# A 12-stage decoder kernel: the side steps of its first cross attention spread over more slots, and semaphores cleared by ranges

## What is computed

```python
q = (x @ Wq + bq).reshape(1, B * N, H, hd)            # B*N = 2048 queries
kv = (cond @ Wkv + bkv).reshape(1, -1, 2, H, hd)      # 512 keys
q, k, v = fq_sym(q * scale), fq_sym(k), fq_sym(v, over the keys)    # 8 bit, kept as floats
attn = softmax(q @ k.T)
attn = clip(round(attn / s), 0, 255) * s               # s = max(attn) / 255, by row
return (attn @ v) @ Wp + bp
```

## Time and profile before

| | us |
|---|---|
| median of 3 runs | 3998.09 (3995.31 to 3998.46) |
| the profiled execution | 3996.9 |
| its span, first to last instruction | 3995.1 |
| of it L0X, from the barrier before it to the one behind it | 277.2 to 664.0 |
| of that the loop, from its first maxima to its last | 307.2 to 643.6 |

### The profile page before, as it was taken

The page is one execution under the profiler, slowest core; times in us unless marked ns, Lnnn a source line. Parts: engine busy times, 40 slices in busy tenths (PEclk is TensorE's granted clock), DMA queues, the critical chain, the costliest instruction groups (busy, mean ns, idle before and its releaser), DMA issues. The chain is left out here.

```text
span 3995.1 us, 56226 instructions
## 1 busy us (share of the span) xinstructions
PE 3152.4 (79%) x17265; PEld 2306.4 (58%) x17296; DVE 2698.2 (68%) x8364; ACT 1820.2 (46%) x5598; POOL 467.9 (12%) x585
## 2 busy tenths in 40 slices
PE   7975554979999997764589974569999999999465
PEld 5653333747777775542267762237777777777344
DVE  4667875368878885668844457856666676666597
ACT  4546664135555552224411122346666666666243
POOL 0011110011111110111111110011111111111100
PEclk9995555989999998776689986679999999999588
DMA  1004555000000001000000012000000000000000
GB/s 57 1 23 88 96 94 143 1 14 1 1 1 1 1 1 40 0 4 26 1 16 1 1 44 103 1 11 1 1 1 1 1 1 1 1 1 1 33 1 22
DMA packets 141736, 83.72 MB, mean 21 GB/s; under 512 B 135424, under 2 KB 139648, under 8 KB 139776
## 3 DMA queue, kind: packets, MB, share of 16 engines
q1 hardware_dynamic: 141440, 80.14, 7.5%
HBM read 44.47 MB, written 2.10 MB: 12 GB/s over the span
## 5 line engine op out<-in xcount | busy, mean ns | idle before, releaser
L2213 DVE CUSTOM_DVE_ANT_0 L3A_masked<-ps,L3A_hidden,L3A_negrstd 128x128 f32<-128x128 f32 (+1 forms) x512 | 193.4, 415 | 322.7 <-PE ps L2104 233.4
L2162 ACT ACTIVATE L3A_probs<-L3A_masked,L3A_negmax 128x128 f32<-128x128 f32 (+1 forms) x512 | 228.8, 449 | 237.3 <-DVE L3A_negmax L2213 237.2
L332 PE MATMUL ps<-s_weights_b,s_XT 128*128 128x512 f32 (+1 forms) x640 | 301.1, 603 | 36.7 <-ACT s_XT L753 12.8
L2132 PE MATMUL ps<-s_weights_b,L3A_OT 128*128 128x256 f32 x1024 | 264.1, 381 | 14.5 <-DVE s_R L2242 14.5
L332 PE MATMUL ps<-s_weights_b,s_Xc 128*128 128x512 f32 x512 | 243.7, 598 | 7.4 <-DVE L3A_rot L2077 3.3
L879 ACT ACTIVATE L0X_pf<-ps,L0X_bias,L0X_qscale 128x512 int16<-128x512 f32 x256 | 197.1, 776 | 114.9 <-DVE L0X_bias L912 113.8
L2085 POOL TENSOR_TENSOR L3A_rstd<-L3A_ve,s_mhalf 128x4 f32<-128x4 f32 x144 | 145.0, 1007 | 852.5 <-DVE L3A_ve L2045 852.5
L332 PEld LDWEIGHTS ps<-s_weights_b,s_XT 128*128 128x128 f32 x640 | 124.0, 211 | 127.4 <-issue 69.3
L909 DVE TENSOR_REDUCE L0X_negmax<-ps 128x2 f32<-128x1024 f32 x128 | 156.1, 1219 | 60.7 <-PE ps L820 59.0
L2132 PEld LDWEIGHTS ps<-s_weights_b,L3A_OT 128*128 128x128 f32 x1024 | 175.1, 191 | 28.9 <-issue 15.7
L2162 ACT ACTIVATE L1A_probs<-L1A_masked,L1A_negmax 128x128 f32<-128x128 f32 (+1 forms) x256 | 114.3, 447 | 119.7 <-DVE L1A_negmax L2213 117.1
(11 more groups left out here) (512 smaller groups left out, 8635.4 us busy)
## 6 DMA issues: line engine op xcount, KB each, us to landing
s_weights_b<-w_L3A SPq DMA_DIRECT2D x1, 9984.0 KB, 26.7
s_weights_b<-w_L1A SPq DMA_DIRECT2D x1, 7936.0 KB, 21.5
s_weights_a<-w_L2F SPq DMA_DIRECT2D x1, 4224.0 KB, 12.9
s_weights_b<-w_L1F SPq DMA_DIRECT2D x1, 3840.0 KB, 11.9
s_weights_b<-w_L3F SPq DMA_DIRECT2D x1, 3136.0 KB, 10.9
s_weights_a<-w_L2A SPq DMA_DIRECT2D x1, 2898.0 KB, 9.6
s_weights_a<-w_L0F SPq DMA_DIRECT2D x1, 2176.0 KB, 8.8
s_X<-x SPq DMA_DIRECT2D x1, 2048.0 KB, 8.3
```

What stands on the lines that cost most here:

```text
L332: last = pe.matmul(out, lhs(k), rhs(k), start=(k == 0), stop=(k == n - 1))
L2132: last = pe.matmul(c.bank(3)[:, j * DM:(j + 1) * DM], OT[:, u % 4, j * P:(j + 1) * P], w["wo"][:, h, :], start=(h == 0 and j == 0), stop=( ...
L2162: last = a.activation(pr[:, u % 4, cols], ms[:, u % 2, cols], ACT.Exp, bias=nmx[:, h, j:j + 1], scale=-1.0, accum_out=sm[:, h, j:j + 1])
L2213: last = eng.tensor_tensor_reduce(out=ms[:, u % 2, cols], in0=s[:, cols], in1=hidden[:, P - j * P:2 * P], scale=-1.0 if gated else nrs[:, ...
```

## The change

Two things. First, `clear` gives GpSimd one instruction for each run of consecutive semaphore numbers, where it had one for each semaphore. Second, in L0X the steps Q and Y are cut in two, by tile of tokens: the first half (Q, Y) tells nobody, the second (Q+, Y+) stands in the next slot and tells VectorE, which does its part for both. All steps get other slots; T1 of a sequence moves into slot 0 of that sequence itself, and its scores wait for T0 only, and for T1 from their second tile on. `outputs` moves from slot 5 to 6, the scaling of the normalised rows from 13 to 15, and GpSimd's parts move accordingly.

```diff
             def _(pool):
-                for s in self.sems:
-                    pool.sem_clear(s)
+                numbers = sorted(s.num for s in self.sems)
+                first = numbers[0]
+                for n, after in zip(numbers, numbers[1:] + [None]):
+                    if after != n + 1:
+                        pool.sem_clear(range(first, n + 1))
+                        first = after
...
-    STEP_AT = {0: ("X", 1), 2: ("Q", 1), 6: ("oT", -1), 8: ("Y", -1), 10: ("T0", 1), 11: ("T1", 1)}
+    STEP_AT = {0: ("T1", 0), 2: ("X", 1), 4: ("Q", 1), 5: ("Q+", 1), 8: ("oT", -1), 10: ("Y", -1), 11: ("Y+", -1), 14: ("T0", 1)}
+    STARTS = ("Q", "Y")
...
-            elif what == "Q":
-                for j in range(TT):
-                    last = project(pe, halves[:, j, :], lambda k: c.XT[:, k, j * P:(j + 1) * P], lambda k: w["wq"][:, k, :])
+            elif what in ("Q", "Q+"):
+                j = len(what) - 1
+                last = project(pe, halves[:, j, :], lambda k: c.XT[:, k, j * P:(j + 1) * P], lambda k: w["wq"][:, k, :])
...
-            last.then_inc(side_made, 1)
+            if what not in STARTS:
+                last.then_inc(side_made, 1)
...
-                    if p % PAIRS == 0:
-                        pe.wait_ge(side_act, act_through(("T1", b)))
+                    if m == 0:
+                        pe.wait_ge(side_act, act_through((("T0", "T1")[j], b)))
...
-                    if i >= 0 and s % PAIRS == VALUE_LAG - 1:
+                    if i >= 0 and s % PAIRS == VALUE_LAG:
                         outputs(i)
-                    if i >= 0 and s % PAIRS == 13:
+                    if i >= 0 and s % PAIRS == 15:
                         S.vec_norm_scale(v, i + 1, i)
```

More of the change, by code:

```diff
@@ L641, in sublayer_l0_cross @@
     VALUE_LAG = 6
-    STEP_AT = {0: ("X", 1), 2: ("Q", 1), 6: ("oT", -1), 8: ("Y", -1), 10: ("T0", 1), 11: ("T1", 1)}
-    VEC_LATER = 1
-    steps = [("X", 0), ("Q", 0), ("T0", 0), ("T1", 0)]
+    STEP_AT = {0: ("T1", 0), 2: ("X", 1), 4: ("Q", 1), 5: ("Q+", 1), 8: ("oT", -1), 10: ("Y", -1), 11: ("Y+", -1), 14: ("T0", 1)}
+    STARTS = ("Q", "Y")
+    steps = [("X", 0), ("Q+", 0), ("T0", 0), ("T1", 0)]
     step_at = {}
@@ L649, in sublayer_l0_cross @@
             i = s // PAIRS + ahead
-            if 0 <= i < SEQS:
+            if 0 <= i < SEQS and (what, i) not in steps:
                 step_at[s] = (what, i)
-                steps.append((what, i))
+                if what not in STARTS:
+                    steps.append((what, i))
     number = {x: m for m, x in enumerate(steps)}
-    BY_ACT, BY_VEC = ("X", "T0", "T1", "oT"), ("Q", "Y")
+    BY_ACT, BY_VEC = ("X", "T0", "T1", "oT"), ("Q+", "Y+")
     def act_through(x):
@@ L721, in pe_side @@
             what, i = x
-            m = number[x]
+            m = number[(what + "+", i) if what in STARTS else x]
             if m:
@@ L742, in pe_side @@
             else:
-                for j in range(TT):
-                    last = project(pe, halves[:, j, :], lambda k: c.oT[:, k, j * P:(j + 1) * P], lambda k: w["wp"][:, k, :])
-            last.then_inc(side_made, 1)
+                j = len(what) - 1
+                last = project(pe, halves[:, j, :], lambda k: c.oT[:, k, j * P:(j + 1) * P], lambda k: w["wp"][:, k, :])
+            if what not in STARTS:
+                last.then_inc(side_made, 1)
         def act_side(a, x):
@@ L766, in vec_side @@
             e.wait_ge(side_made, number[x] + 1)
-            if what == "Q":
+            if what == "Q+":
                 if i:
@@ L841, in _ @@
                             lambda k: ctxT[:, k, :]).then_inc(v_made, 1)
-                for x in steps[:2]:
+                for x in (steps[0], ("Q", 0), steps[1]):
                     pe_side(pe, x)
@@ L956, in _ @@
                         steps_of(s - 2)
-                    if s - VEC_LATER in step_at:
-                        vec_side(v, step_at[s - VEC_LATER])
+                    if s - 1 in step_at:
+                        vec_side(v, step_at[s - 1])
                     i = s // PAIRS - 1
-                    if i >= 0 and s % PAIRS == VALUE_LAG - 1:
+                    if i >= 0 and s % PAIRS == VALUE_LAG:
                         outputs(i)
-                    if i >= 0 and s % PAIRS == 13:
+                    if i >= 0 and s % PAIRS == 15:
                         S.vec_norm_scale(v, i + 1, i)
@@ L991, in _ @@
                     i = s // PAIRS
-                    if s % PAIRS == 4 and i + 1 < SEQS:
+                    if s % PAIRS == 7 and i + 1 < SEQS:
                         pool_q(p, i + 1)
@@ L995, in _ @@
                         if i > 1:
-                            g.wait_ge(side_vec, vec_through(("Y", i - 2)))
+                            g.wait_ge(side_vec, vec_through(("Y+", i - 2)))
                         g.tensor_tensor(Xb[:], c.X[:, i * TT:(i + 1) * TT, :], over(w["bp"], TT), ALU.add).then_inc(xb_ready, 1)
-                    if i and s % PAIRS == 10:
+                    if i and s % PAIRS == 13:
                         S.pool_rstd(g, i - 1)
```

## The result

Medians in us, the two kernels side by side on one chip:

| | before | after |
| --- | --- | --- |
| median of 4 runs (lowest to highest) | 3996.83 (3995.31 to 3998.46) | 3928.7 (3925.62 to 3928.93) |
| span of the profiled execution | 3995.1 | 3923.8 |
| L0X, barrier to barrier | 386.4 | 360.7 |
| its loop, first maxima to last | 336.4 | 312.4 |
| the 23 gaps between sublayers, together | 67.8 | 23.7 |

A forecast was written before the change was run, and what follows sets the result against it. Bounds: in L0X, VectorE's work and its waits for scores; between sublayers, single clears with all other engines waiting. 46.6 (clears) + 19.5 (loop) = 66.1 us off the 3998.1 median gives 3932, within 3924 to 3942 (0.66).

The forecast's parts named there:

- The clears, 46.6 us: Semaphore clears between sublayers: 684 instructions become 46, so 638 go at 0.073 us each, gaining 46.6 us.
- a clear of many numbers takes what a clear of one does: Clears between sublayers: a clear of a range takes 44 ns however wide, so the full 46.6 us are gained.
- Rival 1: Clears cost by width: 27 ns per number gives 3949 us (chance 0.12); the full 0.073 us gives 3978 (0.04).
- The 73 ns for each clear: Blocks of clears: 24 more clears cost VectorE 1.75 us more idle time, 0.073 us each, all on the path.
- rival 2: At the clears: code fetched under them is now waited for, at most 28 us back, 3946 to 3960 (chance 0.05).
- The loop, 19.5 us: L0X: period from 44.2 to about 41.7 us, 18.5 over the loop; with start and rounding, 19.5 in all.
- the seven waits: L0X period: seven small VectorE waits, 0.3 to 1.2 us each, sum 5.6, in place of three of 2 to 3.
- I took 1.2 GHz for all halves: L0X, halves of Q and Y: TensorE's clock rises only at the end of Q+, so a half takes 1.8 us.
- granted clock still near 0.58: Sign for the profile after: the granted clock in the L0X loop stays near 0.58.
- Rival 4: L0X: TensorE runs the halves at 2.4 GHz, 0.95 us each; period 38.4, total 3908 us (chance 0.04).
- Other stages unchanged: Stages other than L0X: unchanged but for the barriers; the prediction calls itself wrong if another stage moves.
- VectorE's three waits for scores: L0X period before: VectorE waits 2.75 us behind Q, 2.62 behind Y, 2.08 behind T1, together 7.45.

## Where the prediction was right and where not

- **The clears, 46.6 us.** Measured 44.2 in the gaps, 45 by the kernel that has them alone. The term that was wrong is "a clear of many numbers takes what a clear of one does": it takes 129 ns at 17 and 259 at 41, and over the 46 clears that is 3.3 us more than 44 ns each. Rival 1 had the direction, but 27 ns for each number; the rows say about 5. From the other side came 0.8 us, since the time from the last clear to the next work got shorter at some places. The 73 ns for each clear held, but not as read: one clear follows the next after 71 ns, and in five of the 23 blocks one step takes 360 to 363 ns, which makes the mean 73. The two blocks of the earlier trace rows have no such step. What these pauses are no run shows; with ranges they are gone. At 17 numbers VectorE's idle time was to be 2.00 - 16 x 0.071 = 0.86 with a free width; the 0.09 of the wide clear make it 0.95, as measured. At 41 it is 3.75 less the 2.88 us of the single clears and plus the 0.38 of the three that replace them, 1.25, and 1.26 was measured.
- **Fetches.** The part around the clears stayed what it was in most places: 0.46 us from the last work to the first clear and 0.34 from the last clear to the next work, in the median of the 23 places, before and after. At three places the second part fell (0.68, 0.78 and 0.63 us before, 0.32 to 0.34 after). At two it grew: from 0.32 to 0.41 in this profile alone, and from 0.32 to 0.54 at the first of the two blocks of 17 clears, those of L3X, in all runs with this `clear`. There the last of the engines to reach the block's end is TensorE (instructions of L177 at this place, before and after):

```profile
L177 PEldq DRAIN  x1: 135/135/135, 3706.2 to 3706.2; - x1
```

```profile
L177 PEldq DRAIN  x1: 135/135/135, 3640.7 to 3640.7; - x1
```

In both it ends 0.42 us behind the start of the first clear. The 17 clears took 1.18 us and covered it; the one clear of 0.13 us does not. So something did come to light, as rival 2 said, but it is 0.22 us at one place and no fetch. What the Trainium skill's section on instruction fetch mechanics ("Runtime: NRT & Kernel Launch") speaks of is not seen at these places: had the 17 clears of the earlier trace rows covered a fetch, VectorE's idle time there would be longer than the 0.95 of the point above, and it is 0.95.
- **The loop, 19.5 us.** Measured 25.7 in the first profile and 22.3 in the second. All of the seven waits are where they were said to be: 0.40, 0.51, 0.72, 1.09 and 1.05 for 0.36, 0.44, 1.14, 0.91 and 1.11 (the third, behind Q, is the worst), and slots 6 and 12 with 0.82 each where the clock is as assumed. Then the period is 42.0 us for 41.7 forecast. The step that failed is "I took 1.2 GHz for all halves": in most periods the clock rises inside Q+ and Y+, which take 1.4 to 1.8 us for 2.07, and those two waits are 0.2 to 0.3. That makes the period 40.95, 0.75 less than forecast, and over the six whole periods 5.1 us, most of the 6.2 that the forecast had too little. The sign "granted clock still near 0.58" failed with it: it is 0.63. The rows had shown a rise behind 4.7 us of busy TensorE, and the step took that one place for the rule. Rival 4 named the mechanism, with too large a size: it had the first half fast as well.
- **`outputs`.** Named as a new cost of 0.91 us a period; it is 1.09, and taking it away gave some 11 us in all, 6 to 9 of them in L0X.
- **Other stages unchanged.** True in the sum (3533.0 to 3531.6), not stage by stage: L1A is 1.2 us shorter and L2X 1.1. By the prediction's own words ("I am wrong if another stage moves") that is a miss. It had no term for TensorE's clock in stages that the change doesn't touch, and these shifts come with it. That they nearly cancel in this kernel is luck; with the loop alone they are 6.6 us.
- **The total.** The forecast of 3932 is 3 us from the 3928.7 measured. The clears had 2.4 us too much and the loop 6.2 too little, so part of this closeness is luck.
- **What bounds the loop.** That VectorE's three waits for scores are what can be gained was the premise. The kernel without them is 55 us shorter in L0X than before and runs at VectorE's pace.

What the prediction didn't ask is whether halves or slots bring the gain. It listed the slots' savings (T1) and costs (`outputs`, X, slot 0) side by side, and by its own numbers they nearly cancel; the kernel with the new slots alone shows it. That the halves in the old slots take most of T1's wait away as well, so that the move of T1 is not needed for it, it did not see.

## What to carry to other kernels

A serial block between stages is worth counting: one instruction for each semaphore, 71 ns apart with four engines standing, was 1.2% of this kernel, and a clear by range costs 44 to 259 ns for any width seen here. In a loop that one engine paces, write down when each side step's input is ready and how long the step blocks the engine that feeds the pacing one. In this loop a step was free when it stood three slots behind the copy it needs and was short enough for TensorE's lead; a whole projection still cost up to 1.0 us there, and cut in two it cost nothing. And look at what a moved consumer now holds up: here one slot later for `outputs` gave back some 11 us.

## What was not expected of the hardware

- A semaphore clear by range costs 44 ns for 1 number, 47 to 53 for four, 64 for five and then about 5.4 ns for each more, up to 259 at 41. Single clears follow each other after 71 ns, but in five of the 23 blocks one step took 0.36 us.
- The clock was not to be foretold from TensorE's own rows here. In the changed kernel it rose inside the second half of a projection (0.50, then 0.77); in another execution of the very same kernel it stayed at 0.50 there for two periods; with the halves in the old slots, TensorE as busy, it stayed at 0.50 as well. In the kernel with whole steps in the best slots TensorE was busy nearly throughout from 373.84 us on, with one stop of 0.37 us, and was still at the lower level 7.9 us later (window of that stretch):

```profile
373.84:381.70 7.86, 7.49 (x52) 5.05 (x52) 7.37 (x17) 7.41 (x18) 0.00 (x0) 0.50 0.66 127
```

- Stages with the same instructions differ by up to 5 us between kernels and repeat within 0.3 us in the two kernels that were profiled twice (L0A and L0X apart). The difference is in TensorE's clock: in L2A it is 0.96 at 281.3 us, 0.95 at 283.8 and 0.94 at 286.5. Such a difference is no work that an edit elsewhere added or took away.
